# A graph network's attention: steps two and three run in 14 pieces inside the dense passes before them, and those passes count 1856 columns instead of 2320

## The reference

```python
terms = [x0]                                 # x for both heads, H = 2
for _ in range(K_ORDER):                     # 4 steps
    prev = terms[-1]
    gcn_i = _gcn_conv(prev, row, col, deg_inv, n)    # segment_sum(prev[row], col) * deg_inv
    attn_i = _attn_conv(qs, ks, prev)                # (qs @ (ks^T prev) + sum(prev)) / (qs . sum(ks) + n)
    terms.append(BETA * gcn_i + attn_i)
xcat = jnp.concatenate(terms, axis=-1).reshape(n, H * C * (K_ORDER + 1))
return (xcat @ Wo_w + Wo_b) / H
```

## Time and profile before

| what | us |
|---|---|
| median of 3 runs | 5326.28 (5324.18 to 5327.95) |
| profiled execution, span | 5325.0 |
| PE busy | 4321.5 (81%) |
| DVE / ACT / POOL busy | 2815.1 (53%) / 1451.2 (27%) / 3251.7 (61%) |
| pass 2, step 2 | 463.61, 79.63 |
| pass 3, step 3 | 462.64, 98.10 |

### The profile page before, as it was taken

The page is one execution under the profiler, slowest core; times in us unless marked ns, Lnnn a source line. Parts: engine busy times, 40 slices in busy tenths (PEclk is TensorE's granted clock), DMA queues, the critical chain, the costliest instruction groups (busy, mean ns, idle before and its releaser), DMA issues. The chain is left out here.

```text
span 5325.0 us, 78049 instructions
## 1 busy us (share of the span) xinstructions
PE 4321.5 (81%) x26640; PEld 3018.0 (57%) x26640; DVE 2815.1 (53%) x7430; ACT 1451.2 (27%) x2914; POOL 3251.7 (61%) x3382
## 2 busy tenths in 40 slices
PE   4677866979868787788879997999889767777786
PEld 3444434545535556554446664666555467667775
DVE  6588886755367776535562315221432444455554
ACT  1377850010057664111120102010210122222222
POOL 2766626767767775075516661776177367777774
PEclk6789988989989999699989998999999898999998
DMA  4265559999933344195588887988697465555553
GB/s 145 45 61 80 91 100 194 199 182 187 202 80 101 104 126 109 60 289 159 168 265 271 270 248 250 280 268 253 228 303 241 130 171 144 143 149 146 151 153 82
DMA packets 1261118, 909.00 MB, mean 171 GB/s; under 512 B 446403, under 2 KB 1181934, under 8 KB 1260638
## 3 DMA queue, kind: packets, MB, share of 16 engines
q1 hardware_dynamic: 909866, 519.09, 39.3%
q0 software_dynamic: 102704, 232.38, 16.1%
q10 hardware_dynamic: 248132, 152.25, 9.9%
HBM read 696.10 MB, written 118.89 MB: 153 GB/s over the span
## 5 line engine op out<-in xcount | busy, mean ns | idle before, releaser
L1687 PE MATMUL ps<-adj_d,xs_d 128*128 128x464 bf16 (+1 forms) x4704 | 992.8, 367 | 60.1 <-DVE xs_d L1648 60.1
L3166 POOL DMA_INDIRECT rows_mg<-p_tab,src_idx x784 | 758.3, 967 | 273.4 <-issue 238.1
L1601 POOL DMA_INDIRECT rows_d<-xh_tab,src_idx x632 | 617.7, 977 | 479.8 <-POOLq L187 207.4
L1601 POOL DMA_INDIRECT rows_d<-x_tab,src_idx x512 | 499.1, 975 | 475.5 <-POOLq L187 264.4
L1687 PEld LDWEIGHTS ps<-adj_d,xs_d 128*128 128x128 bf16 x4704 | 466.1, 101 | 509.1 <-DVE xs_d L1648 61.9
L1295 POOL DMA_INDIRECT rows_d<-h_tab,slot_idx x490 | 497.0, 1014 | 266.9 <-issue 143.9
L2216 POOL DMA_INDIRECT rows_g<-x_tab,src_idx x444 | 434.2, 978 | 164.7 <-issue 127.3
L3263 PE MATMUL ps<-win_mg,turned_hot_mg 128*128 128x128 f32 x1568 | 341.2, 302 | 201.2 <-DVE pre_mg L3215 201.0
L1431 PE MATMUL ps<-adj_d,xs_d 128*128 128x512 bf16 (+1 forms) x2028 | 441.0, 375 | 54.6 <-DVE xs_d L1396 49.9
L1673 PEld LDWEIGHTS ps<-onehot_d,rows_d 128*128 128x128 f32 x3552 | 428.6, 192 | 66.6 <-DVE onehot_d L1619 33.5
L1673 PE MATMUL ps<-onehot_d,rows_d 128*128 128x72 f32 (+1 forms) x3552 | 421.4, 275 | 31.3 <-DVE onehot_d L1619 26.3
(11 more groups left out here) (442 smaller groups left out, 7541.4 us busy)
## 6 DMA issues: line engine op xcount, KB each, us to landing
adj_d<-adjacency SPq DMA_DIRECT2D x140, 812.0 KB
adj_d<-adjacency SPq DMA_DIRECT2D x84, 857.5 KB
attr_mg<-in_edge_attr SPq DMA_DIRECT2D x195, 256.0 KB
xp_g<-x_tab SPq DMA_DIRECT2D x70, 448.0 KB
k_rows_d<-k_tab ACTq DMA_DIRECT2D x56, 448.0 KB
loc_mg<-loc_rows SPq DMA_DIRECT2D x196, 128.0 KB
q_s<-q_tab SPq DMA_DIRECT2D x42, 448.0 KB
rden_s<-rden_tab SPq DMA_DIRECT2D x42, 448.0 KB
```

The lines of the kernel that those rows point to most:

```text
L1601: nc.gpsimd.indirect_dma_start(rows[:, q % GR * K + k, :], None, table, bass.IndirectOffsetOnAxis(ap=src_idx[:, j:j + 1], axis=0)).then_in ...
L1687: last = nc.tensor.matmul(ps[:, m % 2, 0:w], xs[:, g * GW + k, e, :], adj[:, slot, k, 0:w], start=(g == 0 and k == 0 and e == 0), stop=(g ...
L3166: nc.gpsimd.indirect_dma_start(rows[:, q % RR, k, :], None, p_tab, bass.IndirectOffsetOnAxis(ap=src_idx[:, j:j + 1], axis=0)).then_inc(row ...
```

## The change

1. `Split(5, 464, 468)` becomes `Split(4, 464, 416)` for two heads: 56 tiles instead of 70, 368 edge tiles (92 groups) gathered instead of 316 (79).
2. Steps 2 and 3 are no longer stages. `dense_pass` takes a `fused` step: 14 visits of 512 or 384 nodes, each with an `ask` and a `finish`. A visit opens when its columns are stored and their gathered sums are in. `fused_slots` plans all slots ahead with constant costs; five visits stay behind the last tile.
3. The plan puts the 14 pieces of `keys_values` into slots 1 to 14, one in each, where `due` put one into every fifth. The single buffer stays. Groups are placed by a clock, at most two in a slot.
4. Both heads of a group share one bank of `ps` (`sums_of`), and their matmuls are ordered head by head. A visit's buffers lie in `raw`, in the buffers of `keys_values`, in unused weights and in a new `more`.
5. Pass 2 first copies `xT` to memory (`x_kept`, 3.2 MB), for `step_again`, which repeats a step behind a `general_pass` that did run. Step 2 writes to `xh2_tab`, step 3 to `xh_tab`.

The core of the diff:

```diff
-SPLITS = {1: Split(6, 490, 528), 2: Split(5, 464, 468)}
+SPLITS = {1: Split(6, 490, 528), 2: Split(4, 464, 416)}
+TILE_US, GROUP_US, GATHER_US, PIECE_US, VISIT_US = 4.2, 1.75, 5.05, 1.6, 4.3
...
+                        while t < tiles or q < groups or finished < PARTS_N:
+                            took = pieces[p:p + 1] if t else []
+                            opens = p >= len(pieces) and t >= free_at
+                            p += len(took)
+                            group = []
+                            while q < groups and len(group) < 2 and clock > 4.5 + GATHER_US * (q + 1):
+                                group.append(q)
+                                q += 1
...
-                        bank = 2 + heads * (q % 2)
-                        return ps[:, bank:bank + heads, 0:NARROW]
+                        return ps[:, 2 + q % 2, :].rearrange("p (h n) -> p h n", h=heads)[:, :, 0:NARROW]
...
+                def load_rest(self, act, i):
+                    if i < PARTS_N:
+                        c, w = self.visits[i]
+                        if i:
+                            act.wait_ge(self.made, HEADS * i)
+                        act.dma_start(self.share[:, 0:w], dinv_row[c:c + w].partition_broadcast(P)).then_inc(self.rest_in, 16)
+                        for h in range(HEADS):
+                            act.dma_start(self.rden[h][:, 0:w], rden_tab[h * P:(h + 1) * P, c:c + w]).then_inc(self.rest_in, 16)
+                def start(self, act):
+                    if keeps:
+                        act.dma_start(x_kept, xT[:, 0:NP]).then_inc(self.kept, 16)
...
+                    elif eng is nc.vector:
+                        eng.wait_ge(self.rest_in, 16 * (1 + HEADS) * (i + 1))
+                        a = acc[:, 0:HEADS, c:c + w]
+                        nc.vector.tensor_tensor(a, a, self.share[:, 0:w].unsqueeze(1).to_broadcast([P, HEADS, w]), ALU.mult).then_inc(self.scaled, 1)
...
-            dense_pass(f"2{step}", table, heads, SPLITS[heads], phases)
-            general_pass(f"2{step}", table, heads, src_index, dst_target)
-            if step < ORDER:
-                layer2_step(step)
+        for step, table, to, sums in ((2, xh_tab, xh2_tab, G), (3, xh2_tab, xh_tab, PARTS_N)):
+            make = fused_step(step, to, step == 2)
+            dense_pass(f"2{step}", table, HEADS, SPLITS[HEADS], [[keys_values(table, HEADS, 1, sums)]], make)
+            general_pass(f"2{step}", table, HEADS, src_index, dst_target, nodes=step_again(make, step < ORDER - 1))
```

More of the change, by code:

```diff
@@ L45 @@
 BATCH = 14
+NODE_PARTS = [(g * GC + half * BLOCK, GW - BW if half else BW) for g in range(G) for half in range(2)]
+PARTS_N = len(NODE_PARTS)
+Slot = namedtuple("Slot", "pieces groups tile ask finish")
+TILE_US, GROUP_US, GATHER_US, PIECE_US, VISIT_US = 4.2, 1.75, 5.05, 1.6, 4.3
 MOST = 256
@@ L1483, in dense_pass @@
                         at += len(work.signals)
+                    if step:
+                        step.take(*s[at:])
                     tiles = heads * blocks * G
@@ L1497, in ends_at @@
                         return order.index((m, G - 1)) + 1
-                    due, settled = [[] for t in range(tiles + 1)], {}
                     pieces, opened = [], []
@@ L1502, in dense_pass @@
                         opened.append(len(pieces))
[L1503 removed]
+                        most = max(work.parts for work in phase)
                         for g in range(G):
[L1505 to L1507 removed]
@@ L1508, in dense_pass @@
-                    for k, piece in enumerate(pieces):
-                        before = phases[opened.index(k) - 1] if k and k in opened else ()
-                        due[1 + k * (tiles - 1) // len(pieces)].append((before, piece))
-                    gathered = [[] for t in range(tiles + 1)]
-                    for q in range(groups):
-                        gathered[min(tiles, 2 + q * tiles // groups)].append(q)
-                    def beside(eng, t):
-                        for before, piece in due[t]:
+                            for k in range(most):
+                                pieces.append([(work, k, g) for work in phase if work.parts == most] +
+                                              [(work, 0, g) for work in phase if work.parts < most and k == most // 2])
@@ new lines, in dense_pass, with stored_at, needs @@
+                    pieces = [(phases[opened.index(k) - 1] if k and k in opened else (), piece) for k, piece in enumerate(pieces)]
+                    def stored_at(m):
+                        return order.index((m + 1, 2) if m else (1, G - 1)) if m < heads * blocks - 1 else tiles
+                    def needs(c, w):
+                        first_block = (heads - 1) * blocks
+                        covering = [first_block + b for b in range(blocks) if b * block_of < c + w]
+                        g = c // GC
+                        of_dense = c + w <= blocks * block_of
+                        sums = 0 if of_dense else groups if g == G - 1 else max(0, FINAL[g] - tail // K)
+                        return covering[-1] if c < blocks * block_of else -1, sums
@@ L1518, in beside @@
+                    if step:
+                        slots, visits = fused_slots()
+                        step.visit(visits)
+                        begins = min(k for k, slot in enumerate(slots) if slot.ask is not None)
+                    else:
+                        slots = even_slots()
+                    first_idle = min(k for k, slot in enumerate(slots) if slot.tile is None)
+                    def beside(eng, slot):
+                        for before, piece in slot.pieces:
                             for work in before:
@@ L1638, in add @@
                             nc.vector.tensor_tensor(a, a, sums_of(q), ALU.add).then_inc(added, 1)
-                        for t in range(tiles + 1):
-                            if t < tiles and splits_at(t) is not None:
-                                h, g = splits_at(t)
+                        for k, slot in enumerate(slots):
+                            if slot.tile is not None and splits_at(slot.tile) is not None:
+                                h, g = splits_at(slot.tile)
                                 s = h * G + g
@@ L1692, in general_pass @@
+                            if slot.finish is not None:
+                                if slot.tile is None:
+                                    pe.wait_ge(stored, heads * blocks)
+                                step.finish(pe, slot.finish, turn_bank(slot))
+                                finished += 1
         def general_pass(n, table, heads, index, target, weighted=False, nodes=None):
@@ L2509, in _, with keys_values @@
                         sp.wait_ge(k_out, 16 * G + 16)
-        def keys_values(table, heads, slots):
+        def keys_values(table, heads, slots, sums):
             class KeysValues:
```

327 lines of the change are left out of this document (277 added, 50 removed).

## The result

The changed kernel took 5355.69 us (median of 7 runs, 5337.85 to 5366.38) against 5324.83 us of the kernel before in the same comparison: a ratio of 1.0054, 95% interval 1.0042 to 1.0066. It is slower by 0.5%. Forecast were 5281 us and a range of 5236 to 5345, so the measured time lies outside.

The account below looks back on a forecast made before the run. PE's own work was taken to bound passes 2 and 3. 1004.3 us without waits + 2 x 19 + 6 + 2 x 5 = 1058.3, 45.7 less than 1104.0, so 5281 us; range 5236 to 5345.

Parts of the forecast that it names:

- There DVE and a transfer take turns: Five visits behind the last tile: DVE's scaling and the reload alternate; tail 51 us in pass 2, 52.5 in pass 3.
- scaling waiting 5.5 us for `more_d`: Sign in the tail of the changed profile: DVE's scaling (L3028) waits 5.5 us for the `more_d` transfers.
- 3.6 us from the last store to the next stage: End of the tail: time from the last rows' queue entry to the next stage, 3.6 us.
- A pass is PE's own work: Passes 2 and 3: PE's instructions follow without gaps, so work taken from PE is gained if nothing else comes late.
- Slots 1 to 14, one buffer, 9.7 us a slot, 19 us a pass: Pieces wait for their single buffer's load: slots of 9.7 instead of 8.27 us, 13 waits x 1.43 = 19 us a pass.
- slower rival: Single buffer sets the pace in slots 1 to 14: load 10.7 us, slot 12.3, total 5366; chance 0.17.
- The copy of `xT`, 6 us: Pass 2: the 3.2 MB copy stands in ACT's queue ahead of the second load, costing 6 us (0 to 10).
- Up to the last tile 473.5 and 481.3 us: From stage start to the end of PE's last tile, waits included: 473.5 us in pass 2, 481.3 in pass 3.
- POOL hides under this: Passes 2 and 3: 368 gathers take 460 us, last group wanted at about 470; 10 us left, POOL the next bound.
- the 99.7 us: Gain over passes 2 and 3 with their steps if the change added no new waits.
- Nothing else in the kernel changes by more than about 1 us: Outside passes 2 and 3 and their steps, changes of at most about 1 us (52 more edge tiles in preparation).
- 1004.3 us without waits: Both changed stages together without new waits, 494.5 + 509.8 us, against 1104.0 before.

Follow-up runs that it names:

- b2: Changed kernel, but behind the last tile PE runs a slot's two groups ahead of the visit's ask: ratio 1.0042 to the kernel before, fast transfers.
- b1: Changed kernel with the loads of `q` issued one visit earlier: ratio 1.0060 to the kernel before, fast transfers.
- e1: b4 plus the `xT` copy queued at slot 28 and ACT copying turned rows before the sums of values: ratio 0.9987 to the kernel before, fast transfers.
- d3: d2 without the `general_pass` stages behind passes 2 and 3: ratio 1.0117 to the kernel before, slow transfers.
- a4: Changed kernel with the 14 pieces in every second slot (1 to 27): ratio 1.0189 to the kernel before, slow transfers.
- b4: Changed kernel with `q` one visit earlier, groups ahead of the ask and pieces in every second slot: ratio 0.9983 to the kernel before, fast transfers.
- f2: Changed kernel with only its two new tables declared behind all others: ratio 1.0242 to the kernel before, slow transfers.
- e3: Kernel before with only the new split (four blocks of 464, 92 groups) in passes 2 and 3: ratio 1.0078, fast transfers.
- e2: Kernel before with only the changed kernel's layout of tables and buffers: 5335.7 us, one run, fast transfers.
- d0: Kernel before, unedited, profiled again where transfers are slow: 6026 us.
- a1: Kernel before with only the new split in passes 2 and 3, same kernel as e3: ratio 1.0213, slow transfers.
- e0: Kernel before, unedited, profiled again where transfers are fast: pass 1 with step 1 508 us, passes 2 and 3 with their steps 543 and 559.
- d2: Same kernel as e1, run where transfers are slow: ratio 1.0128 to the kernel before.

## Why the prediction was wrong

- *"There DVE and a transfer take turns", five visits behind the last tile in 51 us: this step failed.* With the next term it is 19.5 and 23.3 of the 67 us that the two stages missed by. From scaling to scaling the forecast had 9.3, 8.35, 9.3 and 9.3 us; measured were 9.5, 16.7, 15.7 and 8.7 in pass 2 and 10.9, 15.2, 15.6 and 11.3 in pass 3, 14.3 and 16.6 us more. The row forecast, scaling waiting 5.5 us for `more_d`, came once in pass 2 (3.35) and twice in pass 3 (1.26, 6.91). In its place PE set the two middle cycles: `q` is queued behind the last rows' copies and sums, and PE has two groups behind the ask, at half clock up to 6.91 us. I had read what DVE does in a visit but not what PE and ACT have queued ahead of it. The count shows it too: 92 - 84 = 8 groups were left behind the last tile, and only two of them got a price. b2 shows the groups' part (20 us in the median, 14 in the tails), b1 that `q` alone is not worth it. With both mended, DVE and the reload do take turns (e1): the step named the next limit, not the one that held.
- *3.6 us from the last store to the next stage: mis-sized.* From 3317.20 to 3326.37 it was 9.2 us, and 8.2 in pass 3. The earlier trace rows come from a stage with no empty stage behind it; d3, without that stage, has 2.9 and 2.8.
- *A pass is PE's own work: right.* Its counts and durations stand.
- *Slots 1 to 14, one buffer, 9.7 us a slot, 19 us a pass: the mechanism right, the sum in part luck.* Behind the second piece the slots are 9.6 and 9.7 us long, and the waits all but go when the pieces are spread (a4, b4). But seven waits there make 8.8 and 9.3 us where twelve of 1.43, 17 us, were forecast, as some slots hold more groups and work behind a long wait runs at 1.2 GHz (3.32 us for a piece of 1.73). The second piece makes up for it with 4.28 and 9.23 us: in pass 3 it came 13.3 us after its loads were queued (3345.51 to 3358.82), longer than the slower rival's 10.7. Why the first loads of a pass take that long no run isolates. The slower rival as such, 12.3 us in every slot, was not what happened, although its total, 5366, comes near; where transfers are slow the slots of f2's pass 2 are 11.0.
- *The copy of `xT`, 6 us: wrong in place, and too high.* It held up the second tile's adjacency block by 7.07 us, not the second load alone. Its queue entry also stands ahead of ACT's first cast, and the first tile starts 1.7 us later than in pass 3. Against pass 3, which has no copy, pass 2 lost 7.07 + 4.28 + 1.7 - 9.23 = 3.8 us at this place, and with the copy moved (e1) a wait of 5.13 us came where b4 had the 6.1 of the adjacency block.
- *Up to the last tile 473.5 and 481.3 us: 13.1 and 11.2 too low.* Read so far: the adjacency block's wait, tiles of 5.70 to 6.78 us behind waits instead of 4.28, and asks waiting for ACT's copies (4.8 us in pass 2). The rest isn't divided.
- *POOL hides under this: half right.* In the changed kernel yes: its last gather starts at 3282.18, 44 us before the next stage. But with the split alone it bounds (e3), and with the waits repaired its rows come 2 to 3 us late (b4). Whether all of the 99.7 us could be had is not shown.
- *"Nothing else in the kernel changes by more than about 1 us": not borne out by the profiles,* 18 us, of which up to 9 may be that the longest run was profiled. Some 12 us lie within what two profiles of the kernel before differ by in pass 1; e2 puts up to 13 us on the layout alone. How it divides is not settled.

Together: against 1004.3 us without waits the two stages took 1125.5, 121 more. 78 of these lie up to the last tile, where 54 were forecast (31.6 are the pieces' waits, 7 the adjacency block's), and 43 in the tails, where none were. So 99.7 us of gain became 21.6 of loss, and the other stages added 18 in this profile.

## What to carry to other kernels

When a stage is folded into another, its last part, with nothing left to hide under, has to be worked out queue by queue: for each engine what stands ahead of the instruction that the next cycle waits for, at the clock that engine has after idling. A wait that is removed may only uncover the next one: here the reload behind `q` and the groups, and the second piece's load behind the copy. Cutting work of the engine that bounds pays only up to the next engine's own time (here POOL's 470 us), so run the cut alone first. And before a difference in a stage whose code nobody touched is put down to the change, profile the old kernel twice; here one kernel differed by 12 us from itself.

## What was not expected of the hardware

- Two kinds of chip: 5325 and 6016 us for one kernel, with 165 and 132 to 133 GB/s from pass 4 on. The same change costs 0.5 to 0.8% on one and 2.4% on the other. Whether it is the chip or something else that used its memory, no run tells.
- On the slow kind PE had gaps of 0.3 to 1.8 us with nothing to wait for, 16 us in groups and tiles of pass 2 of the kernel before (d0) and 59 in the split alone (a1); on the fast kind (e0, e3) none of this sort. The profile shows no cause.
- The granted clock may or may not fall behind equal idle times (3.29 us: a tile of 4.51 or 6.19 us, one kernel, two profiles).
- At a nearly equal busy share of the DMA engines the first 60 us of pass 1 moved 318 GB/s in the three fast profiles with the old layout and 292 to 302 in the seven with the new.
- A stage that does nothing cost 5 to 6 us between two others (d3 against d2).
